# A mixture-of-experts block: first-weight rounding moved to ScalarE, gating and residual of results moved to VectorE

## What is computed

```python
score = softmax(xf @ Wg + bg); gate = max(score); idx = argmax(score)     # one expert for each token
pos = (cumsum(onehot) - 1) at idx; keep = pos < 512                       # an expert takes at most 512 tokens
h = relu(einsum('ecd,edh->ech', buf, W1) + b1)                            # 512 -> 2048
y = einsum('ech,ehd->ecd', h, W2) + b2                                    # 2048 -> 512
out = where(keep, y[idx, pos] * gate, 0)
x = x + gb * out                                                          # gb: one row of 512 for each batch
```

## Time and profile before

| | |
|---|---|
| time, median of 3 | 1845.41 us (1844.32 to 1848.64) |
| profiled execution | 1845.4 us, span 1843.8 us |
| PE busy | 98% of the span |
| DVE busy | 63% |
| ACT busy | 45% |
| POOL busy | 44% |
| mean granted PE clock | 0.99 |

### The profile page before, as it was taken

How to read it: one execution, slowest core, us unless ns; L and a number is a source line. 1 busy time by engine, 2 the same in 40 slices (tenths; PEclk the granted TensorE clock), 3 DMA queues, 4 the chain that set the end, 5 groups by cost and what they waited for, 6 DMA issues and landing times.

```text
span 1843.8 us, 28129 instructions
## 1 busy us (share of the span) xinstructions
PE 1799.0 (98%) x9131; PEld 1494.0 (81%) x9132; DVE 1169.9 (63%) x1875; ACT 830.5 (45%) x1330; POOL 805.1 (44%) x681
## 2 busy tenths in 40 slices
PE   8999999999999799999999999998998999999997
PEld 3688888888888378889888888887888888888886
DVE  4478788788887554546635454557558786455762
ACT  2554655645545333443423333345456454343542
POOL 2144555455464412335424232336547765233542
PEclk9999999999999899999999999999999999999999
DMA  8386777777687534344344434345345544435522
GB/s 285 131 237 163 191 198 171 187 188 189 184 200 216 124 115 145 122 151 179 130 166 143 160 128 142 120 156 215 137 169 187 214 180 169 145 119 175 212 83 69
DMA packets 148300, 304.08 MB, mean 165 GB/s; under 512 B 17969, under 2 KB 18365, under 8 KB 146198
## 3 DMA queue, kind: packets, MB, share of 16 engines
q1 hardware_dynamic: 114970, 221.01, 34.1%
q0 software_dynamic: 33280, 82.42, 18.5%
HBM read 254.29 MB, written 67.43 MB: 174 GB/s over the span
## 4 chain that ended last, share of the span: by engine, by line
PE 85%; DVE 3%; issue 2%; POOL 1%; DMA 1%; ACT 1%; DVEq 0%; ACTq 0%; POOLq 0%
PE bank L332 26%; PE bank L334 25%; PE bank L333 25%; PE bank L734 3%; PE bank L813 1%; PE bank L600 1%; PE bank L894 1%; PE bank L726 1%; POOL yo L1864 0%; DMA out_dram<-yo,tok_x 0%; DVE h_lo L1614 0%; PE bank L704 0%; DMA xh<-h_rows,tok_h 0%; PE bank L709 0%; ACT h_f L1222 0%
## 5 line engine op out<-in xcount | busy, mean ns | idle before, releaser
L1614 DVE TENSOR_TENSOR h_lo<-h_f,h_hi 128x512 fp32r<-128x512 f32 x256 | 222.9, 891 | 361.9 <-ACT h_f L1222 241.7
L1221 ACT ACTIVATE h_hi<-bank,b_col 128x512 fp32r<-128x512 f32 x256 | 176.4, 689 | 598.0 <-PE bank L334 470.8
L332 PE MATMUL bank<-bt_hi,w_hi 128*128 128x512 f32 (+4 forms) x1024 | 361.0, 353 | 8.4 <-DVE w_lo L1587 5.5
L333 PE MATMUL bank<-bt_lo,w_hi 128*128 128x512 f32 (+4 forms) x1024 | 359.2, 351 | 0.0
L334 PE MATMUL bank<-bt_hi,w_lo 128*128 128x512 f32 (+4 forms) x1024 | 359.1, 351 | 0.0
L332 PE MATMUL bank<-w_hi,h_hi 128*128 128x512 f32 x832 | 325.8, 392 | 0.7 <-issue 0.6
L333 PE MATMUL bank<-w_lo,h_hi 128*128 128x512 f32 x832 | 324.2, 390 | 0.0
L334 PE MATMUL bank<-w_hi,h_lo 128*128 128x512 f32 x832 | 324.0, 389 | 0.0
L332 PEld LDWEIGHTS bank<-bt_hi,w_hi 128*128 128x128 f32 x1024 | 194.4, 190 | 34.8 <-issue 9.8
L333 PEld LDWEIGHTS bank<-bt_lo,w_hi 128*128 128x128 f32 x1024 | 194.5, 190 | 21.2 <-issue 0.2
L334 PEld LDWEIGHTS bank<-bt_hi,w_lo 128*128 128x128 f32 x1024 | 194.4, 190 | 20.2
(11 more groups left out here) (280 smaller groups left out, 3104.5 us busy)
## 6 DMA issues: line engine op xcount, KB each, us to landing
raw<-in_L_ffn_W_dram SPq DMA_DIRECT2D x128, 1024.0 KB
xa<-in_L_attn_x_dram SPq DMA_DIRECT2D x16, 1024.0 KB, 8.0
xr<-in_L_attn_x_dram SPq DMA_DIRECT2D x16, 1024.0 KB, 6.5
h_rows<-sb_tab SPq DMA_DIRECT2D x16, 1024.0 KB, 11.5
xr<-global_rows POOLq DMA_DIRECT2D x16, 1024.0 KB, 8.6
out_dram<-xr SPq DMA_DIRECT2D x16, 1024.0 KB, 9.7
h_rows<-h POOLq DMA_DIRECT2D x16, 1024.0 KB
b_bc<-in_L_ffn_b_dram SPq DMA_DIRECT2D x16, 256.0 KB, 6.4
```

The costliest lines, as they stand in the source:

```text
L332: pe.matmul(o, a_hi, b_hi, start=start, stop=False)
L333: pe.matmul(o, a_hi, b_lo, start=False, stop=False)
L1221: act.activation(h1_hi[b % 2][:, j, :], h_bank[j][:, :], ACT.Relu, bias=bias)
L1614: dve.tensor_tensor(h1_lo[b % 2][:, j, :], h1_f[:, j, :], h1_hi[b % 2][:, j, :].bitcast(F32), ALU.subtract) \
```

## The change

In the experts, the rounding of each W1 block goes from VectorE to ScalarE, where it stands behind the first `relu` of the block before (`w1_high`); VectorE keeps the low part (`w1_low`). The gating and the residual of expert e-1's rows go from GpSimd to VectorE (`gate_results`), behind `result_rows` in b = 0: four multiplications, then four additions. GpSimd keeps its gathers and scatters.

```diff
+        def w1_high(n, e, b):
+            act.wait_ge(w1_in[b % 2], 16 * (NB // 2 * e + b // 2 + 1))
+            wait_past(act, h1_full, 4 * n - 4)
+            act.activation(w1_hi[b % 2][:], raw[2 * (b % 2)][:], ACT.Copy).then_inc(w1_hi_done, 1)
...
                 relu(e, b, 0)
+                if b + 1 < NB:
+                    w1_high(n + 1, e, b + 1)
+                elif not last:
+                    w1_high(n + 1, e + 1, 0)
                 relu(e, b, 1)
...
-        def split_w1(n, e, b):
-            dve.wait_ge(w1_in[b % 2], 16 * (NB // 2 * e + b // 2 + 1))
-            wait_past(dve, h1_full, 4 * n - 4)
-            dve.tensor_copy(w1_hi[b % 2][:], raw[2 * (b % 2)][:]).then_inc(w1_hi_done, 1)
+        def w1_low(n, b):
             dve.wait_ge(w1_hi_done, n + 1)
             dve.tensor_tensor(w1_lo[b % 2][:], raw[2 * (b % 2)][:], w1_hi[b % 2][:].bitcast(F32), ALU.subtract) \
                 .then_inc(w1_split, 1)
...
+        def gate_results(e):
+            dve.wait_ge(gb_gated, 4 * e + GS)
+            dve.wait_ge(xo_in, 16 * GS * (e + 1))
+            for i in range(GS):
+                q, j = 4 * e + i, GS - 1 - i
+                dve.wait_ge(y_taken, q + 1)
+                dve.tensor_tensor(yo[:, j, :], yo[:, j, :], gb_rows[:, j, :], ALU.mult).then_inc(y_scaled, 1)
+            for i in range(GS):
+                q, j = 4 * e + i, GS - 1 - i
+                dve.wait_ge(y_scaled, q + 1)
+                dve.tensor_tensor(yo[:, j, :], yo[:, j, :], xo[:, j, :], ALU.add).then_inc(y_ready, 1)
...
                 if b == 0 and not first:
                     result_rows(e - 1)
+                    gate_results(e - 1)
...
         def finish_rows(e):
-            pool.wait_ge(xo_in, 16 * GS * (e + 1))
             for i in range(GS):
                 q, j = 4 * e + i, GS - 1 - i
-                if not (isinstance(e, int) and e == E - 1):
-                    pool.wait_ge(gb_gated, 4 * e + j + 1)
-                    pool.wait_ge(y_taken, q + 1)
-                    pool.tensor_tensor(yo[:, j, :], yo[:, j, :], gb_rows[:, j, :], ALU.mult).then_inc(y_scaled, 1)
-                    pool.wait_ge(y_scaled, q + 1)
-                    pool.tensor_tensor(yo[:, j, :], yo[:, j, :], xo[:, j, :], ALU.add).then_inc(y_ready, 1)
                 pool.wait_ge(y_ready, q + 1)
```

More of the change, by code:

```diff
@@ L1678, in expert @@
                 split_hidden(e, b, 0)
[L1679 to L1682, removed]
+                if not (last and b == NB - 1):
+                    w1_low(n + 1, (b + 1) % 2)
                 for j in range(1, HC):
```

## The result

The changed kernel takes 1849.1 us (median of 13 runs, 1846.48 to 1855.1), the kernel before 1845.7 us beside it (13 runs, 1844.32 to 1848.64). The ratio is 1.0018, with a 95% interval of 1.0011 to 1.0025: slower by 0.18%. That it is slower is clear of the noise; that it is slower by less than the 0.2% that the prediction counts as no change is so for the median, but the interval reaches beyond it. The forecast was 1845.8 with a range from 1838 to 1849.5. The profiled execution took 1847.76 us, with a span of 1846.2, against 1845.4 and 1843.8 before.

The account below looks back on a forecast made before the run. PE, busy 98%, was taken as the bound, with some 15 us of waits and clock to win. Gains of 1.9 + 3.5 + 0.6 less 0.4 gave 1839.8; two clock falls added 6.0: 1845.8 us, range 1838 to 1849.5.

Parts of the forecast that it names:

- range of 8 in 10: Whole kernel: 1838 to 1849.5 us, held to contain the time with 8 chances in 10.
- the forecast's own range: Whole kernel with two clock falls: 1843.4 to 1848.6 us, by a fall's two prices and 1 us for each seam's steps.
- the seam waits: Ends of experts 7 and 9: PE waits 3.7 us for ScalarE's last `relu` ahead of the transposes, instead of 1.76 and 2.03.
- the falls of the clock: Seams of experts 7 and 9: PE's clock falls to half in both waits, costing 3.0 us each, 6.0 together.
- rival (d): Seams: W1 comes later still; 1.7 us more at each makes it slower by over 0.2%, 2.5 gives 1850.8; chance 0.14.
- Hidden(2) and hidden(3): Expert 7, time less 1200: hidden(2) starts at 57.7, not 57.98; hidden(3) at 66.5 without a wait, 3.1 us sooner.
- Relief and added work on VectorE: Expert 7, time less 1200: undisturbed `h_lo` and `w_lo` cancel against eight more operations; `w1_low` ends at 56.8, before 56.9.
- The waits for `bt_lo`: After expert 7's seam: tokens' low part no longer late, so the 0.94 us wait ahead of the next hidden(0) goes.
- the load's 9.5 us: Seams of experts 7 and 9: the two loads and b2 take 9.5 us; expert 7's W1 at 70.5, time less 1200.
- rival (b): Seams: GpSimd's scatters leave earlier, the load is in time, the wait is 2.8 us; 1838.0 with no fall; chance 0.07.
- (a): Seams of experts 7 and 9: clock falls once, 1842.8 us, chance 0.15, or not at all, 1839.8 us, chance 0.08.
- (c): Whole kernel: VectorE's relief is all that counts, ScalarE takes the rounding with no wait behind it; 1830.4 us, chance 0.04.

Follow-up runs that it names:

- Experiment 5: The changed kernel with each scatter writing 16 of its 512 columns to a scratch array, the experts' contribution to the output left out: 1844.79 us.
- experiment 1: The changed kernel with gating and residual back on GpSimd, so that only the rounding moves to ScalarE: 1855.07 us.
- experiment 6: The changed kernel with 15 extra matmuls, result unused, ahead of the transposes in experts of one tile: 1846.24 us.
- experiment 2: The changed kernel with the rounding (CAST) left on VectorE, so that only gating and residual move: 1841.44 us.
- experiment 11: The changed kernel with VectorE rounding each next expert's first W1 block and W1 of block b+3 loaded ahead of W2 of block b+2: 1843.21 us.
- experiment 12: The changed kernel with all rounding left on VectorE and W1 of block b+3 loaded ahead of W2 of block b+2: 1839.36 us.
- experiment 4: The changed kernel with W1 of block b+3 loaded ahead of W2 of block b+2: 1841.96 us.
- experiment 3: The changed kernel with VectorE rounding the first W1 block of each next expert, ScalarE the other 48: 1842.09 us.
- experiment 9: The changed kernel with a VectorE fill of 64 columns ahead of each of five operations of block 1: 1846.37 us.
- experiments 7 and 8: The changed kernel with W1 loaded earlier and token and gate copies moved to block 3: 1867.52 us; also with VectorE rounding each next expert's first block: 1865.58 us.

## Why the prediction came out right

The forecast of 1845.8 us lies 3.3 us under the median of 1849.1. The median is inside the range of 8 in 10 by 0.4 us and outside the forecast's own range of 1843.4 to 1848.6. The mechanism was the one that the prediction walked through, and two of its terms were off in opposite directions: the seam waits came 2.2 and 2.5 us longer than 3.7, and the falls of the clock 1.5 and 0.8 us cheaper than 3.0. That the second error made up for half of the first is luck. With the falls at the price of the forecast, the same waits give an estimate of 1849.1 + 2.3 = 1851.4 us, which is in rival (d) and outside the range.

**Hidden(2) and hidden(3).** The changed kernel enters expert 7 1.0 us late (hidden(0) at 1232.50, not 1231.50). Less this 1.0, hidden(2) starts at 57.8 (forecast 57.7) and hidden(3) at 66.4 without a wait (66.5). Relief and added work on VectorE cancel as summed; three `h_lo` take 1.96 us and the mean `w_lo` 2.29. The waits for `bt_lo` and ahead of hidden(2) of expert 11 went as forecast.

**The seam: mechanism right, the load mis-sized.** The transposes start at 79.17 - 1.0 = 78.2, where the forecast had 76.2. W2 and W1 were issued 3.14 us after hidden(2)'s start (forecast 3.3), so the 2.0 us are the load's: 11.6 instead of 9.5. Experiment 5 shows that the scatters' bytes make 1.8 of it, experiment 1 that with GpSimd's arithmetic between the scatters the load takes 9.6. The mis-sized term is the load's 9.5 us, taken over from before. Behind it stands the step "GpSimd's scatters now leave earlier" in rival (b): within expert 7 the first is issued 5.7 us later than before and is then held by VectorE, and the other three leave together, beside the load. Rival (d) priced this very lateness (from 1.7 us more at each seam the kernel is slower by over 0.2%), for another reason (gathers), and it came at 2.0.

**The clock: both falls came, below their price.** The forecast took a fall as 3.0 us, from expert 9 of before, where PE works 5.7 us of it. In the changed kernel both falls last 6.8 us again. In expert 7, 3.8 of them lie inside the wait, PE works 3.1 us at 1.2 GHz and loses 1.5 us. In expert 9 the clock falls at 1405.1, only 2.0 us lie inside the wait, PE works 4.8 us at 1.2 GHz and loses 2.2 us (experiment 6). The Trainium skill, TensorE: Matmul & The Clock Gate, section "Why this matters for your kernels", says to keep PE from idling between bursts; the trace agrees, with 5.85 and 6.20 us of waiting and a fall in each. How short a wait must be to be safe, the prediction took from one trace, in which 3.34 us cost the clock and 2.21 did not. Other traces put no line there: the clock fell within 1.5 us after waits of 2.12 and 2.02 us in experiment 2, of 2.03 in experiment 11 and of 2.17 in experiment 12, and did not fall at one of 2.84 in experiment 4.

**The sum.** Expert 7, from its hidden(0) to expert 8's, takes 52.71 us instead of 51.56: 1.15 lost, forecast 1.1. The load's 2.0 more and the clock's 1.5 less nearly cancel there. Experts 8 and 9 lose 0.8 (forecast: 0.5 gained). Experts 10 and 11 gain 1.1 (forecast 0.6), the rest loses 0.5 (0.4). With the 1.0 us from ahead of expert 7 that is 2.4, as the spans say. This 1.0 stands in no step: 0.7 of it is there at the first wait in the experts (740.11, before 739.43). That place lies between 739 and 744 us in the traces of the other versions too, whose work ahead of it is the same or nearly so, so I put it down to the spread of single executions; this is argued, not shown.

**The rivals.** (a) did not come. (b) has it the wrong way round. (c), at 1830.4, is far: ScalarE is 51% busy and still held PE for 4 us at each seam. That rounding on ScalarE takes load off VectorE is true (63 CASTs of 1.41 us), and won nothing here: where VectorE does the seam's rounding (experiment 3) or all of it (experiment 2), the kernel is 7 to 8 us faster than the changed one.

That a scatter with nothing ahead of it on GpSimd leaves at once did not hold. The Trainium skill, SBUF — State Buffer, section "Who interferes with whom", which the prediction used for the relief, says that a software-issued DMA seen stalling beside VectorE was starved while GpSimd made its descriptors. It also says that `tensor_tensor`, which is the operation here, was not seen to stall a DMA. On this second point the traces differ from it, with 6.39 us beside the unbroken stretch and 1.78 with a break (experiment 9), and the measurement decides.

## What to carry to other kernels

Before an operation is put into another engine's in-order queue, look at what it waits for in its worst place, not at the engine's busy share: 61 of 63 roundings waited for nothing, and the two that waited for a load held three `relu`s and PE. Taking work off an engine can bring its DMAs together: ask which transfers they will then run beside, and price the load with them in it. When a change has two halves, time each alone, and look where each gains and loses: here one half was worth 4 to 5 us, and the other cost 8 for the most part in an expert where the whole change loses nothing.

## What the runs showed of the hardware that I had not expected

A GpSimd scatter stays in issue while VectorE runs operations with two operands in its memory back to back: 5.2, 6.4 and 8.6 us beside stretches of different length, 6.41 with 1/32 of the bytes, 1.78 where a fill of 0.11 us broke the stretch. With the CAST of 1.22 us in the stretch (experiment 2) it takes 3.5 us and ends 0.9 us after the CAST's end, so whether the CAST itself lets it through is not shown.

A fall of the clock costs only what PE works in it: 1.5 us where PE works 3.1 us of it, 2.2 where it works 4.8, an estimated 2.8 where it works 5.7. The falls of the changed kernel are equally long (6.8 us each).

Twelve gathers 1.3 us apart (experiments 7 and 8) go with stops of up to 1.7 us in PE's stream that no semaphore explains, while in the changed kernel ordinary loads at 377 GB/s (1268 to 1272) stop nothing.
